# An agents' stage rebuilt ahead of four interleaved streams: sums' columns, masks, rows and step sequences

## The chip, the cores and the metric

The kernel runs on one core of one Trainium2 chip. The metric is the device time of one execution, in microseconds (us). The trace is one execution taken by the hardware profiler on that core. The engines are PE (TensorE matmuls; PEld is its loading of stationary operands), DVE (VectorE), ACT (ScalarE), POOL (GpSimd) and SP (SyncE), which here only issues DMAs. Each engine runs its own instructions in order and waits on semaphores for the others.

## The reference

Six layers with a residual and a layer norm after each, over x (32 batches, 100 tokens, 256 channels) and a context (32, 361, 256), all float32:

```
x = LN(x + L0_attn(x))              # the agents' layer
x = LN(x + L0_xattn(x, ctx, masks)) # cross attention with cell_mask and seq_mask
x = LN(x + L0_ffn(x))               # gate, top half of the tokens, 16-head attention
x = LN(x + L1_attn(x))              # banded 16-head attention
x = LN(x + L1_xattn(x, ctx))        # cross attention
x = LN(x + L1_ffn(x))               # quantised linear layer
```

The agents' layer is the one that the change rebuilds:

```
agent      = einsum('bnc,c->bn', q, w_conv1)            # one number a token
agent_attn = softmax(einsum('bn,bnc->bc', agent * scale, k))
agent_v    = softmax(einsum('bc,bnc->bn', agent_attn, v))
agent_v    = einsum('bn,bnc->bc', agent_v, v)           # one row of 256 a batch
agent_tok  = softmax(agent[:, :, None], axis=-1)
return agent_tok * agent_v[:, None, :]
```

The masks enter the first cross attention as `scores + log(cell_mask) + log(seq_mask)`.

## The kernel before, in words

**Streams and turns.** The 32 batches make 16 pairs. Four streams A, B, C, D take one pair each in a turn, and there are four turns. Each stream has its own SBUF tiles and its own two PSUM banks. A turn of a stream goes through the stages mix (adds the agents' rows, layer norm), first (cross attention with masks), pick (top half), local (banded attention), second (cross attention) and quant.

**Order.** For each engine a stream is a generator that yields after a step or a few. Strings of letters in `ORDER`, written out by a planner, say for PE, DVE, ACT, POOL and SP whose step is issued next. An engine works strictly in that order, so a step that waits holds up all that stand behind it.

**The agents' stage** comes before all turns and treats all 32 batches together. It has its own list of steps on each engine (`AGENT_TENSOR`, `AGENT_SCALAR`, `AGENT_VECTOR`), which the code calls by name:
- `w`: the vector w_q w_conv1, spread over the partitions (L299).
- `x0` to `x15`: tokens of four batches at a time (a "slot", eight slots) arrive by DMA and are transposed by PE (L320), two steps a slot; ACT copies them out. On DVE `ag0` to `ag7` give the agent numbers of a slot.
- `y0` to `y7`: the sums over tokens, agent times token, as rows (L327, output in four groups of 32 partitions); `row1` copies the four banks out (half on ACT, half on DVE); `yT1` turns the rows into columns (`rows_to_columns`, L307) and DVE copies them.
- `key`, `kmax`, `kexp`, `krec`, `kn`: scores of the first softmax, its maximum, exponential, reciprocal and division; `arT` transposes the result (L344), `z` multiplies by w_v (L349), and `log` gives the logits of the second softmax (L362).
- `lmax`, `lexp` (eight exponentials, L647), `lrec`, `ln` (L855 to L858): the second softmax; `col` turns it into columns (L385), `u0` to `u7` weigh the tokens again (L392), `row2`, `yT2` (L307 again) and `vec` give the agents' vector, copied out as step `v` (L871).
- `p0` to `p6`: products of weights that later stages use (L299, L354, L369, L374, L380), with a scaled copy each on DVE (L820, L822). They need nothing of the tokens.

After `v`, SP stores the 32 rows to DRAM (L1275), waits, and loads each stream's pair of rows over 100 partitions (L1225).

**Masks.** There is one room for the cell mask and one for the sequence mask (`cell`, `seq`), shared by all streams. POOL multiplies the two (L1158), DVE makes the "is zero" part and clips (L891, L893), ACT takes the logarithm (L665), POOL adds (L1162). The next stream's masks are loaded after that (L1229, L1230). So the four streams' masks of a turn follow one another. In the first turn they stand at the start of each stream's steps.

**POOL at the start.** It waits for `u7`, clears rows of the streams' work tiles (L1111, step `rows`, for which ACT and DVE wait before their turns), then clears the value tiles (L1117, L1118, step `zeros`).

## Time and profile before

| | us |
|---|---|
| median of 3 runs | 1081.24 |
| lowest and highest | 1078.39, 1082.4 |
| the profiled execution, its time | 1081.67 |
| its span in the trace | 1079.9 |
| PE busy in the span | 900.4 |
| DVE, ACT, POOL busy | 704.7, 514.2, 371.4 |

How to read it: "busy" counts time in which an engine has an instruction in work; matmuls overlap and their ends are modelled. The page's slices cut the span in 40 equal parts of 27 us; a digit is tenths. A window's row gives the stretch, its length, each engine's busy time with the number of instructions, the clock of PE that was granted (1.00 is 2.4 GHz, 0.50 is 1.2 GHz), the share of 16 DMA engines that was busy, and GB/s. A timeline's row gives start, duration (first start to last end), engine, line, operation, tiles, shape and count; in brackets the idle time before it and what ended that. An operation's row by source line gives count and the least, the median and the largest duration in ns. In the trace one f32 product of the kernel is two matmul instructions, a transpose one.

### The profile page before, as it was taken

Reading aid. Unit: us, or ns where it says so; the run is one execution under the profiler, and the core shown is the slowest. Engines: PE = TensorE matmul, PEld = TensorE weight load, DVE = VectorE, ACT = ScalarE, POOL = GpSimd, SP = SyncE. Lnnn points to the kernel's source line nnn. Section 1 sums busy time; section 2 is a strip of 40 time slices with the busy share of each in tenths; the row PEclk is TensorE's granted clock in tenths of the full one; section 3 lists DMA queues with packets and bytes.
Section 4 is the critical chain, followed back from the end, with each engine's and each line's share of the span. In section 5 each row is a group of like instructions: output and inputs, shape, how many; then the busy total and the mean of one; then the engine's idle time right before and its main releaser. Section 6 shows DMA issues by size and latency. Waiting matters only on the chain.

```text
span 1079.9 us, 19738 instructions
## 1 busy us (share of the span) xinstructions
PE 900.4 (83%) x7022; PEld 671.0 (62%) x7022; DVE 704.7 (65%) x2081; ACT 514.2 (48%) x2392; POOL 371.4 (34%) x528
## 2 busy tenths in 40 slices
PE   7957798898798699998889788897979688997983
PEld 5735677565577587665567566574647466765662
DVE  4235666565777857567697876558487686766576
ACT  3102244766542345865433355664535144556641
POOL 0045401344463322254443422236144232223243
PEclk9766898999888799997889699898869898998896
DMA  7801400002214000002032200011030400000000
GB/s 227 285 32 44 157 1 2 2 8 85 92 55 144 24 1 2 2 23 73 30 123 75 78 9 2 12 69 34 11 102 1 144 17 1 1 2 1 1 1 31
DMA packets 23382, 54.10 MB, mean 50 GB/s; under 512 B 3696, under 2 KB 9588, under 8 KB 23284
## 3 DMA queue, kind: packets, MB, share of 16 engines
q1 hardware_dynamic: 23284, 52.84, 14.7%
q8 instruction: 55, 0.90, 0.3%
q14 instruction: 43, 0.35, 0.1%
HBM read 49.53 MB, written 3.31 MB: 49 GB/s over the span
## 4 chain that ended last, share of the span: by engine, by line
PE 50%; DVE 26%; ACT 10%; POOL 5%; issue 4%; DMA 4%; SPq 1%; DVEq 0%; POOLq 0%; ACTq 0%
PE psum L419 8%; PE psum L424 8%; PE psum L458 7%; ACT work L763 4%; PE psum L444 4%; DVE bn L878 4%; PE psum L578 4%; PE psum L589 3%; ACT work L728 3%; DVE x L885 3%; PE psum L599 2%; DVE mx L1040 2%; PE psum L581 2%; DVE res L945 1%; DVE mv L880 1%
## 5 line engine op out<-in xcount | busy, mean ns | idle before, releaser
L763 ACT ACTIVATE work<-psum,mx 100x100 f32<-100x100 f32 x512 | 169.8, 369 | 53.1 <-DVE mx L1040 52.8
L1124 POOL TENSOR_SCALAR ve<-mv 100x2 f32<-100x2 f32 x96 | 21.7, 226 | 289.7 <-DVE mv L880 289.4
L763 ACT ACTIVATION_READ_ACCUMULATOR work<-psum,mx 100x1 f32 x512 | 118.5, 232 | 0.0
L657 ACT ACTIVATE xT<-psum 128x100 f32<-128x100 f32 (+3 forms) x144 | 53.0, 374 | 124.5 <-PE psum L594 55.9
L458 PE MATMUL psum<-eT,ctx 128*128 128x100 f32 x768 | 103.6, 292 | 7.0 <-DVE eT L914 6.7
L458 PEld LDWEIGHTS psum<-eT,ctx 128*128 128x128 f32 x768 | 99.6, 207 | 10.5 <-DVE eT L914 8.9
L1153 POOL COPY work<-rden 100x128 f32<-100x128 f32 (+1 forms) x80 | 25.1, 314 | 201.4 <-DVE rden L1044 172.6
L444 PE MATMUL psum<-ctxT,qT 128*100 128x361 f32 x256 | 92.6, 508 | 2.1 <-ACT qT L657 1.2
L657 ACT ACTIVATE eT<-psum 100x400 f32<-100x400 f32 (+3 forms) x128 | 64.1, 513 | 49.1 <-PE psum L617 21.2
L878 DVE BATCH_NORM_STATS2 bn<-res 100x6 f32<-100x256 f32 x192 | 82.1, 427 | 6.6
L1040 DVE TENSOR_REDUCE mx<-psum 100x4 f32<-100x400 f32 x128 | 66.9, 565 | 26.4 <-PE psum L581 26.2
L589 PE MATMUL psum<-ident,work 100*100 100x100 f32 x512 | 71.8, 273 | 14.1 <-ACT work L763 13.8
L885 DVE TENSOR_SCALAR x<-res,mv,rstd 100x256 f32<-100x256 f32 x160 | 73.5, 504 | 13.4 <-POOL rstd L1126 13.0
L728 ACT ACTIVATE work<-psum,mx 128x50 f32<-128x50 f32 x256 | 73.8, 349 | 16.4 <-DVE mx L999 16.3
L589 PEld LDWEIGHTS psum<-ident,work 100*100 100x100 f32 x512 | 54.5, 140 | 30.3 <-ACT work L763 22.8
L1126 POOL TENSOR_TENSOR rstd<-ve,minus_half 100x2 f32<-100x2 f32 x96 | 69.3, 722 | 8.0
L578 PE MATMUL psum<-kT,qT 64*100 64x400 f32 x256 | 64.5, 583 | 6.7 <-DVE aT L1051 6.6
L444 PEld LDWEIGHTS psum<-ctxT,qT 128*100 128x100 f32 x256 | 44.4, 181 | 36.0 <-issue 8.0
L1146 POOL TENSOR_TENSOR kT<-work,heads 128x400 f32<-128x400 f32 x64 | 54.4, 853 | 32.9 <-DVE work L1029 32.9
L728 ACT ACTIVATION_READ_ACCUMULATOR work<-psum,mx 128x1 f32 x256 | 63.3, 253 | 0.0
L1046 DVE COPY eT<-psum 100x400 f32<-100x400 f32 x64 | 35.5, 554 | 38.1 <-PE psum L589 37.8
L414 PE MATMUL psum<-ident,x 100*128 100x100 f32 x192 | 31.9, 294 | 28.7 <-DVE x L885 28.6
(231 smaller groups left out, 2066.3 us busy)
## 6 DMA issues: line engine op xcount, KB each, us to landing
ctx<-in_ctx SPq DMA_DIRECT2D x16, 768.0 KB, 7.0
ctxT<-in_ctxT SPq DMA_DIRECT2D x16, 722.0 KB, 4.3
cell<-in_cell SPq DMA_DIRECT2D x16, 282.0 KB
seq<-in_seq SPq DMA_DIRECT2D x16, 282.0 KB
x<-in_x SPq DMA_DIRECT2D x16, 200.0 KB
eT<-agent_rows SPq DMA_DIRECT2D x16, 200.0 KB
out<-xplus SPq DMA_DIRECT2D x16, 200.0 KB
work<-in_x SPq DMA_DIRECT2D x4, 400.0 KB
```

The costliest lines, as they stand in the source:

```text
L419: last = e.matmul(dst, w[:, c, h * P:(h + 1) * P], n(c), start=c == 0, stop=c == NC - 1)
L424: last = e.matmul(dst, xT(c), w[:, c, :], start=c == 0, stop=c == NC - 1)
L444: last = e.matmul(bk[b][0:S, 0:S2], s.qT[:, c, b * S:(b + 1) * S], s.ctxT[:, b, c, :], start=c == 0, stop=c == NC - 1)
L458: last = e.matmul(bk[b][:, c * S:(c + 1) * S], s.ctx[:, b, j, c * P:(c + 1) * P], s.pT[:, b, j, :], start=j == 0, stop=j == S2C - 1)
L578: e.matmul(bk[g][0:S, 0:4 * S], s.qT[r:r + 64, c, b * S:(b + 1) * S], s.keys[r:r + 64, i % 2, :, :], start=True, stop=False, skip_group_ch ...
L589: last = e.transpose(bk[g][0:S, q * S:(q + 1) * S], s.e[:, 4 * g + q, :], ident[0:S, 0:S])
L657: return e.activation(dst, src, ACT.Copy, **kw)
L728: last = e.activation(s.e_pick[:, 4 * g + i, j, 0:CAP], bk[g][:, at_:at_ + CAP], ACT.Exp, bias=s.mx[:, h:h + 1], accum_out=s.den[:, h:h + 1])
L763: last = e.activation(s.e[:, h, :], bk[g][0:S, q * S:(q + 1) * S], ACT.Exp, bias=s.mx[0:S, h:h + 1], accum_out=s.den[0:S, h:h + 1])
L878: e.bn_stats(s.bn[:, b, :], s.res[0:S, b, :]).then_inc(*dve.up(f"bn{b}"))
L885: e.tensor_scalar(dst[0:S, b, :], s.res[0:S, b, :], s.mv[:, b, 0:1], s.rstd[:, b:b + 1], ALU.subtract, ALU.mult).then_inc(*dve.up(f"x{b}"))
L1040: e.tensor_reduce(s.mx[0:S, 4 * g:4 * g + 4], bk[g][0:S, 0:4 * S].rearrange("p (h k) -> p h k", k=S), AX, ALU.max, negate=True).then_inc(* ...
```

## The change

1. *Sums' columns while tokens arrive.* The rows `y0` to `y7` and their turn into columns go. PE makes one column for each batch and half of the channels, with the batch's tokens as the stationary operand (`weighed`), a slot behind the transposes.
2. *Order of the agents' steps.* Only `p0` and `p2` stay ahead of the logits; `p1`, `p3` follow them, `p4` follows `u7`, `p5` and `p6` come last.
3. *Second softmax.* The maximum is subtracted by DVE (`sub0`, `sub1`), ACT takes two exponentials instead of eight; the division is done on the final vector, with a sum from one more matmul (`sum`, `rsum`).
4. *Masks of the first turn.* They are loaded early, into each stream's own tiles (`mask_rooms`), and worked on in the agents' stage: products first thing on POOL, clips on DVE after `row2` (A, B) and after `yT2` (C, D), logarithms on ACT after `row2`, sums on POOL. POOL's `rows` come after the sum of D.
5. *Agents' rows.* `agent_v` stays in SBUF; each batch's row is read from its partition by a DMA of its own over 100 partitions, eight in the first turn.
6. *Loads.* Constants in three groups (`ld_c`, `ld_first`, `ld_const`); the context of C and D after the agents' rows. The zeros of the value tiles move into POOL's first turn.
7. *Sequences.* All five strings of `ORDER` are new.

```diff
-AGENT_TENSOR = ("w " + " ".join(f"x{n}" for n in range(16)) + " " + " ".join(f"y{n}" for n in range(8))
-                + " yT1 key p0 p1 arT z p2 p3 log p4 p5 p6 col " + " ".join(f"u{n}" for n in range(8)) + " yT2 vec")
+AGENT_TENSOR = ("w x0 x1 " + " ".join(f"x{2 * n} x{2 * n + 1} y{n - 1}" for n in range(1, 8)) + " y7 key p0 arT z p2 log p1 p3 "
+                "col sum " + " ".join(f"u{n}" for n in range(8)) + " p4 yT2 vec p5 p6")
...
+            def weighed(i, weights):
+                for j in range(ROWS):
+                    b = ROWS * i + j
+                    for c in range(NC):
+                        last = e.matmul(psum[:, 7, c * B + b:c * B + b + 1], x_of(b)[:, c * P:(c + 1) * P],
+                                        weights[:, b:b + 1], start=True, stop=True)
+                return last
...
-                last.then_inc(*agent_pe.up(f"y{i}"))
-            e.wait_ge(*agent_act("row1"))
-            e.wait_ge(*agent_dve("row1"))
-            rows_to_columns().then_inc(*agent_pe.up("yT1"))
...
+                if i:
+                    e.wait_ge(*agent_dve(f"ag{i - 1}"))
+                    weighed(i - 1, ag).then_inc(*agent_pe.up(f"y{i - 1}"))
...
-            e.wait_ge(*agent_dve("lmax"))
-            for i in range(SLOTS):
-                last = e.activation(l_rooms[i // 4][:, i % 4, :], psum[:, i // 4, i % 4 * P:i % 4 * P + S], ACT.Exp,
-                                    bias=lstat[:, 0, i:i + 1], accum_out=lstat[:, 1, i:i + 1])
+            for k in range(2):
+                e.wait_ge(*agent_dve(f"sub{k}"))
+                last = e.activation(l_rooms[k], l_rooms[k], ACT.Exp)
...
+            for s in streams:
+                masks_log(e, s, 0)
...
+            for s in streams[2:4]:
+                masks_clip(e, s, 0)
             e.wait_ge(*agent_pe("vec"))
-            e.tensor_copy(agent_v, psum[0:B, 6, 0:D]).then_inc(*agent_dve.up("v"))
+            e.tensor_scalar(agent_v[:, :], psum[0:B, 6, 0:D], astat[:, 3:4], None, ALU.mult).then_inc(*agent_dve.up("v"))
+            product(wqk[:, :, :].rearrange("p c n -> p (c n)"), 5, 5)
+            product(wvo[:, :, :].rearrange("p c n -> p (c n)"), 4, 6)
+            e.wait_ge(ld_first, LD_FIRST)
...
         def gpsimd_agents(e):
+            for s in streams:
+                masks_product(e, s, 0)
+            for s in streams:
+                masks_sum(e, s, 0)
+            e.wait_ge(*SD.gpsimd["mask"]("sum", 0))
             e.wait_ge(*agent_pe("u7"))
             for s in streams:
                 last = e.memset(s.work[32 * (ROWS - 1):P, 0:H * HALF], 0.0)
             last.then_inc(*agent_pool.up("rows"))
...
         def load_agent(e, s, t):
-            e.dma_start(s.agent.rearrange("p b d -> p (b d)"),
-                        agent_rows[s.pair(t):s.pair(t) + 1, :].to_broadcast([S, NB * D])).then_inc(s.load_agent.sem, 16)
+            for b in range(NB):
+                n = NB * s.pair(t) + b
+                e.dma_start(s.agent[:, b, :], agent_v[n:n + 1, :].unsqueeze(1).to_broadcast([1, S, D])).then_inc(s.load_agent.sem, 16)
...
             e.wait_ge(*agent_dve("v"))
-            e.dma_start(agent_rows.rearrange("n (b d) -> (n b) d", b=NB), agent_v).then_inc(agent_kept, 16)
-            e.wait_ge(agent_kept, 16)
             for s in streams:
                 load_agent(e, s, 0)
+            for s in (SC_, SD):
+                load_ctx(e, s, 0)
...
     "DVE": (
-        "AAABBAABAACCABCABABABADDCACDBBCCABBADDBABCDCCBDACBABDCDACDABDDBCDCBACABDADDCABDACABABDCABCADBABDCABA"
+        "DBACABDCAABCBADCBDACABCBADCABDACBABCDADBCDBACDCBADBACDBCAACDBADBADCBBCDABCABCADBADABDBABCCDABCABACBD"
```

## Rows read from the trace of the kernel before

**Rows 1.** The page: span, PE's clock in 40 slices, one group of instructions.
```profile
span 1079.9 us, 19738 instructions
...
PEclk9766898999888799997889699898869898998896
...
L657 ACT ACTIVATE eT<-psum 100x400 f32<-100x400 f32 (+3 forms) x128 | 64.1, 513 | 49.1 <-PE psum L617 21.2
```

**Rows 2.** Windows of the fill and of the turns.
```profile
83.00:95.00 12.00, 8.68 (x20) 5.27 (x20) 7.00 (x10) 2.61 (x7) 6.32 (x5) 0.61 0.15 45
...
83.06:200.00 116.94, 98.47 (x771) 79.20 (x772) 69.94 (x223) 50.32 (x234) 36.43 (x43) 0.86 0.13 46
200.00:1000.00 800.00, 686.68 (x5395) 508.04 (x5399) 552.88 (x1602) 415.31 (x1972) 293.56 (x420) 0.89 0.12 41
...
400.00:500.00 100.00, 91.36 (x856) 67.38 (x857) 64.50 (x186) 65.64 (x339) 37.86 (x54) 0.98 0.07 25
```

**Rows 3.** Transposes by source line in three stretches, and windows of two of them.
```profile
6.70:22.30 15.60, 12.81 (x69) 10.39 (x72) 12.21 (x66) 7.57 (x15) 0.00 (x0) 1.00 0.84 261
...
98.00:101.20 3.20, 3.20 (x17) 3.20 (x17) 0.00 (x0) 0.35 (x1) 3.20 (x3) 0.50 0.00 0
...
L320 PE MATMUL psum<-ident,work x32: 374/374/430, 6.7 to 13.3; 100*128 100x100 f32 x32
...
L414 PE MATMUL psum<-ident,x x4: 374/374/374, 100.3 to 100.8; 100*128 100x100 f32 x4
...
L414 PE MATMUL psum<-ident,x x4: 249/276/308, 111.0 to 111.4; 100*128 100x100 f32 x4
```

**Rows 4.** L307 on PE's timeline, whole and its last 19, and a window.
```profile
29.41 5.54 PE L307 MATMUL psum<-ident,v 128*128 128x4 f32 x32 [0.92 <-DVE v L813]
...
30.85 4.10 PE L307 MATMUL psum<-ident,v 128*128 128x4 f32 x19
...
31.00:33.00 2.00, 2.00 (x11) 2.00 (x11) 0.00 (x0) 0.00 (x0) 0.00 (x0) 0.50 1.02 337
```

**Rows 5.** PE's timeline: the transposes of the last tokens.
```profile
20.71 1.59 PE L320 MATMUL psum<-ident,ctxT 100*128 100x100 f32 x8 [1.10 <-DMA ctxT<-in_x]
```

**Rows 6.** PE's timeline around the agent's softmax.
```profile
38.98 1.91 PE L299 MATMUL psum<-res,c_bk_c 128*128 128x256 f32 x4
41.84 0.31 PE L344 MATMUL psum<-ident,kT 32*128 32x32 f32 x2 [0.95 <-DVE kT L840]
```

**Rows 7.** DVE's and PE's timelines, from the logits to their columns.
```profile
49.39 0.99 DVE L848 TENSOR_REDUCE kT<-psum 128x8 f32<-128x800 f32 x1 [4.29 <-PE psum L362]
...
54.73 1.06 DVE L858 TENSOR_TENSOR qT<-qT,kT 128x400 f32<-128x400 f32 x2
...
55.84 1.58 PE L385 MATMUL psum<-ident,qT 128*100 128x4 f32 x16 [1.99 <-DVE qT L858]
```

**Rows 8.** Timelines of POOL, DVE and ACT, from `u7` to the first turn.
```profile
63.14 3.90 POOL L1111 MEMSET work<- 32x1024 f32 x4 [62.70 <-PE psum L392]
...
69.91 0.23 DVE L869 COPY kT<-psum 128x64 f32<-128x64 f32 x1 [4.65 <-PE psum L307]
...
77.95 0.54 DVE L893 TENSOR_SCALAR cell<-cell 100x722 f32<-100x722 f32 x1
78.40 0.48 DVE L945 SCALAR_TENSOR_TENSOR res<-eT,tok,x 100x256 f32<-100x256 f32 x1
78.60 0.81 ACT L665 ACTIVATE cell<-cell 100x722 f32<-100x722 f32 x1 [17.12 <-DVE cell L893]
...
79.49 2.01 POOL L1162 TENSOR_TENSOR kT<-cell,kT 100x722 f32<-100x722 f32 x1 [2.22 <-ACT cell L665]
...
80.42 0.18 DVE L880 BATCH_NORM_AGGREGATE mv<-bn 100x2 f32<-100x6 f32 x1
...
81.76 0.71 POOL L1126 TENSOR_TENSOR rstd<-ve,minus_half 100x2 f32<-100x2 f32 x1
```

**Rows 9.** A window while the agents' rows are loaded.
```profile
76.00:78.00 2.00, 0.00 (x0) 0.00 (x0) 0.59 (x2) 0.00 (x0) 1.27 (x1) 0.50 0.59 207
```

More of the change, by code:

```diff
@@ L92 @@
 GPSIMD = {
+    "start": "zeros",
     "mask": "prod sum",
@@ L351, in tensor_agents @@
             last.then_inc(*agent_pe.up("z"))
-            spread(4, cols["c_bv"], W["c_o"]).then_inc(*agent_pe.up("p2"))
-            for c in range(NC):
-                last = e.matmul(psum[:, 5, 0:1], cols["c_bk"][:, c:c + 1].to_broadcast([P, P]), cols["c_bq"][:, c:c + 1],
-                                start=c == 0, stop=c == NC - 1)
-            last.then_inc(*agent_pe.up("p3"))
+            spread(5, cols["c_bv"], W["c_o"]).then_inc(*agent_pe.up("p2"))
             e.wait_ge(*agent_dve("zT"))
@@ L371, in tensor_agents @@
             last.then_inc(*agent_pe.up("p4"))
+            e.wait_ge(*agent_act("row2"))
+            e.wait_ge(*agent_dve("row2"))
+            for c in range(NC):
+                for i in range(SLOTS):
+                    at_ = (c * SLOTS + i) * ROWS
+                    last = e.matmul(psum[:, 7, at_:at_ + ROWS], u_rooms[i // 2][:, i % 2, c * P:(c + 1) * P],
+                                    ident[:, 0:P:32], start=True, stop=True)
+            last.then_inc(*agent_pe.up("yT2"))
+            e.wait_ge(*agent_dve("yT2"))
+            for c in range(NC):
+                last = e.matmul(psum[0:B, 6, 0:D], yT[:, c, :], W["w_v0T"][:, c, :], start=c == 0, stop=c == NC - 1)
+            last.then_inc(*agent_pe.up("vec"))
+            e.wait_ge(*agent_dve("p3"))
             for h in range(NC):
@@ L623, in tensor_turns, with masks_log @@
                 yield
+        def masks_log(e, s, t):
+            part = mask_rooms(s, t)[0]
+            e.wait_ge(*s.vector["mask"]("clip", t))
+            e.activation(part, part, ACT.Ln).then_inc(*s.scalar["mask"].up("ln"))
         def scalar_agents(e):
             e.preload_act_table_set("natural_log_exp_and_others")
-            def row(name, first, last_, scale):
-                for k, after in ((0, first), (1, last_)):
-                    e.wait_ge(*agent_pe(after))
-                    last = e.activation(y_rooms[k].rearrange("p i d -> p (i d)"), psum[:, k, :], ACT.Copy, scale=scale)
-                last.then_inc(*agent_act.up(name))
             for n in range(NC * SLOTS):
@@ L661, in tokens_columns @@
                 copy(s.xT[:, :, :].rearrange("p c t -> p (c t)"), bk[0][:, 0:NC * T]).then_inc(*act.up("xT"))
-            def masks(t):
-                e.wait_ge(*s.vector["mask"]("clip", t))
-                e.activation(cell[:, :, :], cell[:, :, :], ACT.Ln).then_inc(*s.scalar["mask"].up("ln"))
             def cross(t, stage, bq):
@@ L808, in vector_agents @@
             e.tensor_tensor(tokd, ag, ag, ALU.subtract).then_inc(*agent_dve.up("tokd"))
-            def row(name, first, last_, scale):
-                for k, after in ((2, first), (3, last_)):
-                    e.wait_ge(*agent_pe(after))
-                    last = e.tensor_scalar(y_rooms[k].rearrange("p i d -> p (i d)"), psum[:, k, :], scale, None, ALU.mult)
-                last.then_inc(*agent_dve.up(name))
             def product(dst, k, n, other=None):
@@ L861, in vector_agents @@
+            product(wqbk[:, :], 4, 1)
+            product(bqbk[:, :], 5, 3)
             e.wait_ge(*agent_pe("col"))
             e.tensor_copy(acol, psum[0:S, 7, 0:B]).then_inc(*agent_dve.up("acol"))
-            row("row2", "u5", "u7", 1.0)
-            e.wait_ge(ld_const, LD_CONST)
+            e.wait_ge(*agent_pe("sum"))
+            e.reciprocal(astat[:, 3:4], psum[0:B, 6, D:D + 1]).then_inc(*agent_dve.up("rsum"))
+            for k, ready in ((2, "u5"), (3, "u7")):
+                e.wait_ge(*agent_pe(ready))
+                last = e.tensor_copy(u_rooms[k][:, :, :].rearrange("p i d -> p (i d)"), psum[:, k, :])
@@ L865, in vector_agents @@
+            last.then_inc(*agent_dve.up("row2"))
+            product(bqk[:, :], 4, 4)
+            for s in streams[0:2]:
+                masks_clip(e, s, 0)
             e.tensor_scalar(bq4[:, :], cols["a_bq"][:, :], HEAD_SCALE, None, ALU.mult)
@@ L1112, in gpsimd_agents @@
             last.then_inc(*agent_pool.up("rows"))
-            e.wait_ge(*agent_pool("rows"))
-            e.wait_ge(*agent_dve("w8"))
-            e.wait_ge(*agent_pe("yT2"))
-            for s in streams:
-                e.memset(s.v_pick[:, :, :, :], 0.0)
-                last = e.memset(s.v[:, :, :, :], 0.0)
-            last.then_inc(*agent_pool.up("zeros"))
+            e.wait_ge(ld_first, LD_FIRST)
         def gpsimd_turns(e, s):
```

325 lines of the change are left out of this document (156 added, 169 removed).

## The prediction

> **What bounds the kernel now.** I read the page first. PE is the busiest engine, and its slices of granted clock drop below full speed often [rows 1]. The windows cut the span in three. Up to 83.06 us the agents' stage runs alone. From 83.06 to 200 the four streams fill up: PE is busy 98.5 of 116.9 us at a mean clock of 0.86, so it does 84.7 us of full-clock work. From 200 to 1000 it is busy 686.7 of 800 at 0.89, or 0.764 us of full-clock work per us [rows 2]. At that rate the work before 200 would have taken 110.9 us, so the fill loses only 6.0 us. This is the first thing to see. The masks that come one after the other look bad (the first chain waits for them: PE is busy 8.7 of 12 us at 0.61 [rows 2]), but freeing them can give back about 6 us, not the 40 us by which the streams start apart.
>
> The second thing is the level of PE's clock while the tokens arrive. The clock slices say 9 there, but the matmuls say otherwise. The transposes of that stage take 374 ns each. The same form takes 374 ns where the granted clock is 0.50 (1.2 GHz), and 249 ns at the least where it is 1.00 (2.4 GHz) [rows 3]. So the stage runs at 1.2 GHz. I trust the durations over the slices.
>
> The third is the price of a matmul with few columns. In the turn of rows into columns (L307), 32 of them take 5.54 us, and the 19 that start after 30.85 take 4.10, which is (4.10 - 0.35) / 18 = 0.208 us apart at clock 0.50. The 13 before them start in 30.85 - 29.41 = 1.44 us, 0.111 apart [rows 4]. The load of the 128 stationary columns sets this, so a single column costs as much as four.
>
> **The change, part by part.**
>
> *Sums' columns while tokens arrive.* The 64 matmuls that made rows (L327, 22.3 to 28.6), their copies, and the 32 of L307 go. In their place stand 64 products, one column each, with the tokens as stationary operand. Every f32 product of this kernel is two instructions in the trace (16 calls of L307 are x32), so 128 instructions. They stand in PE's queue between the transposes. The last tokens arrive at 20.7 us; eight transposes take 1.59 us [rows 5], so (1.59 - 0.37) / 7 = 0.17 each. New PE work: 64 x 0.17 + 128 x 0.208 = 10.9 + 26.6 = 37.5 us from 6.7 us, plus 0.5 us for the second group of tokens and some 0.4 us of turnover. The last sum is there at 45.2 us. The old one was there at 29.41 + 5.54 = 34.95 [rows 4]: **+10.2 us**. The transposes wait behind these products, but nobody wants them before the logits. Bounds: below, the products cost what the transposes with the same stationary tile cost (0.17), which takes 4.9 us off; above, 0.208. I take the upper one, since L307's form is nearest.
>
> The Trainium skill ("TensorE: Matmul & The Clock Gate", LDWEIGHTS) has a load of 128 columns take 107 ns whatever the contraction. By it the products would cost 128 x 0.107 = 13.7 us, 12.9 less. The row of L307 at the low level, 0.208, disagrees for f32, and the row decides.
>
> *Agent's softmax.* p1 leaves the path: its four matmuls (38.98, 1.91 us) stood before the transpose of the normalised row at 41.84 [rows 6]. That starts 2.6 us sooner relative to the key. Against this, p0 is dense for only half as long, and before, the clock rose to 1.00 after p0 and p1. I let z, p2 and the logits run at the low level: 8 x 0.1 + 4 x 0.2 + about 1 for the logits, less 0.5 for p3, is +2.1, an estimate from the two spacings (bounds 0 and 3). Net -0.5.
>
> *Second softmax.* From the logits' end (49.39) to the columns (55.84) it was 6.45 us: eight exponentials, then DVE was late with p6 and two products of 0.53 [rows 7]. Now: maximum 0.99, two subtractions of about 0.55, the second exponential of 400 columns 0.51 [rows 1], waits 0.2, so 2.8 us. p1 and p3 lie under it. **-3.6 us.** The missing division moves to a scalar of the last copy. The sum over tokens adds 0.3, and p4 (eight matmuls of one column, 0.9 us at full clock by L307's spacing) stands where only a copy of 0.6 stood: +0.3. Copies, u and the second turn into columns stay.
>
> So far 10.2 - 0.5 - 3.6 + 0.6 = +6.7 us: the agents' vector is there 6.7 us later, near 79.
>
> *Masks of the first turn and zeros.* POOL idled 62.7 us before L1111 [rows 8], so the four products cost nothing; without that cover 1.7 us each. But the tail of the chain is now on the path. DVE clips C and D after the columns' copy (done at 70.14 before, 76.8 now): four of 0.54, done at 79.0. ACT takes the logarithm, 0.81. POOL adds C, then D (2.0 at most each), near 82.3, and only then clears the streams' rows, which took 3.90 [rows 8] when they lay under the second turn into columns. ACT and DVE wait for this signal before any turn: 86.3. Two other chains end close by. PE's p5 and p6 are 16 matmuls at (1.91 - 0.63) / 3 = 0.43 us at the low level, 6.9 us after 79, then 0.7 on DVE: 86.6 at worst. The agents' rows are eight DMAs: issue 8 x 0.4, and the bytes of before moved at 207 GB/s (0.82 MB in 4 us [rows 9]) after some 1.3 us: 85 to 86. DVE's first turn thus starts at 86.4 where it started at 78.40: +8.0. The HBM hop that falls away (about 1.5 us) is hidden behind the other two. If DVE's clips and POOL's sums slow each other, up to 3 more.
>
> *New sequences.* DVE's now begins D, B, A, C. A mix takes 2.2 us. Two others before A's are 4.4; C's before A's normalisation covers POOL's two steps (1.0 with the wait, 81.46 to 82.47) and costs 1.2; A no longer waits for its mask's sum (79.49 + 2.01 against 80.6 [rows 8]), -0.9. PE's first transpose of a stream: 83.06 + 8.0 + 4.7 = 95.8, **+12.7 us**. From there all four streams are ready within 3 us and no mask is waited for. The 6.0 us of fill come back, less some 2.0 for the first 5 us at the low level (0.43 a us against 0.764): **-4.0 us**. Context of C and D is issued behind the agents' rows at about 84 and needs 11 us at the rate of A's and B's: it is wanted after 98, hidden. The zeros now stand in POOL's turns, 1.4 a stream in 20 us that have room.
>
> The rest of the sequences changes everywhere. No row prices that: 989 us of turns keep their work. I take nothing, with +-1% as bounds. PE's last eight steps are all of D, where C and D ended together; up to 5 us of loss.
>
> **Sum.** 1079.9 + 12.7 - 4.0 = 1088.6 us of span. The profiled execution took 1081.67, 1.8 more than its span; the median 1081.24 is 0.4 less. So 1088.6 + 1.8 - 0.4 = **1090.0 us**, slower by 0.8%.
>
> **Rivals.**
> *The turns run denser (faster).* With four streams ready at once and no mask between them, PE may run its first 100 us as it did from 400 to 500: 91.4 busy at 0.98, 0.90 a us against 0.764 [rows 2]. That is 100 x (0.90 / 0.764 - 1) = 17.5 us: 1090 - 17.5 = 1072.5. It decides from 14 us on. For it: PE waits for nobody else there. Against: before, the streams' distance is what mixes their stages, and now they start in step.
> *PE at full clock while tokens arrive.* Then all of it costs half: a group of 8 transposes and 16 products 2.4 us, more than the tokens' arrival still, and the sums end near 28.5: -16.7, so 1073. Against it: the transposes kept PE busy 12.8 of 15.6 us and the level stayed low; L307's back-to-back products let it fall from 1.00 [rows 3, 4].
> *The agents' rows come one packet at a time.* Each DMA reads one partition a hundred times. Before, the source was DRAM: 0.59 of 16 engines for 2 us moved 414 KB, 0.046 us of an engine per KB [rows 9]. In series, 800 KB take 37 us instead of 4. D's rows are the last issued and the first that DVE wants, so all turns wait: up to +32, and 1090 + 32 = 1122. Nothing in the trace reads one partition so; one row of DRAM read a hundred times was no bottleneck.
> The Trainium skill ("SBUF — State Buffer", the DMA port swizzle) gives a port 27.2 GB/s and puts partitions 0 to 3 behind one port: 0.82 MB would take 30 us, some 25 more than I count, 1115 us. No row here shows it.
> *The change only trades.* Denser turns by half of the above: 1081.
>
> **Chances.** Forecast 0.44 (own range 1083 to 1097); denser turns 0.15; only trades 0.12; full clock 0.07; rows in series 0.22 (wholly or in part, 1100 to 1122). The range 1070 to 1115 leaves out about 0.15. 0.5% is about what a measurement can tell, 1075.8 to 1086.6. Faster: 0.15 and 0.07 less their upper edges, 0.19. Same: 0.12, 0.10 of the forecast's low side, and those edges, 0.24. Slower: 0.57.
>
> **What would show it.** Products of one column 0.2 us apart between transposes of 374 ns; the sums' copy on DVE near 45; the vector's copy near 79; clear of rows on POOL from 82; DVE's first mix at 86 and released by POOL (if by the agents' DMA and near 115, the series rival); PE's first transposes near 96; then PE busy over 90% to 150. I am wrong if the level is 1.00 in the token stage, or if the windows after 200 move by over 1%.

## The result, and the profile after

The changed kernel takes 1112.47 us (median of 4 runs: 1104.71, 1105.9, 1119.05, 1120.25) against 1081.1 for the one before on the same chip: ratio 1.0297, interval 1.025 to 1.0345. The profiled execution took 1104.71 us, its span is 1102.9, 23.0 more than before. The forecast was 1090.0; the time lies in the forecast's range, but by the rival with the agents' rows in series and not by the case that I held likeliest.

Columns are those of before: start, duration, engine, line, operation, tiles, shape, count, and idle time with its releaser. First the page, to set against [rows 1].

```profile
span 1102.9 us, 19819 instructions
...
PEclk7675889999898889999899998998969969999696
```

PE's timeline of the token stage and around the agent's vector, to set against [rows 4 to 7]:

```profile
9.78 1.87 PE L314 MATMUL psum<-qT,work 100*128 100x1 f32 x16
...
15.52 1.57 PE L327 MATMUL psum<-ident,work 100*128 100x100 f32 x8
16.88 3.46 PE L314 MATMUL psum<-qT,work 100*128 100x1 f32 x16
...
35.63 6.87 PE L314 MATMUL psum<-qT,ctxT 100*128 100x1 f32 x32
...
111.89 1.56 PE L425 MATMUL psum<-ident,x 100*128 100x100 f32 x8 [36.74 <-DVE x L900]
```

The products of one column stand between the transposes, 3.46 us for 16. The last ends at 42.50 (before: 34.95). What no row of before resembles is the last line: PE idles 36.7 us before the turns' first transposes, which start at 111.89 instead of 83.06. DVE's timeline says for what:

```profile
70.65 0.47 DVE L883 TENSOR_SCALAR agent_v<-psum,vs 32x256 f32<-32x256 f32 x1
...
75.18 0.69 DVE L830 TENSOR_SCALAR wvo<-psum 128x512 f32<-128x512 f32 x1 [1.45 <-PE psum L411]
...
102.90 0.48 DVE L950 SCALAR_TENSOR_TENSOR res<-eT,tok,x 100x256 f32<-100x256 f32 x1 [27.03 <-DMA eT<-agent_v]
...
111.36 2.66 DVE L900 TENSOR_SCALAR x<-res,mv,rstd 100x256 f32<-100x256 f32 x5
```

The vector is there at 70.65, 1.5 us *earlier* than before (72.15). Then DVE waits 27.03 us for a DMA, and does 8.5 us of residuals and statistics of all four streams before it normalises one. The DMA queue's own timeline (SP) and the window of the stretch:

```profile
71.15 23.21 SPq L1241 DMA_DIRECT2D eT<-agent_v  x8
94.40 3.94 SPq L1250 DMA_DIRECT2D ctxT<-in_ctxT  x1
98.39 2.97 SPq L1252 DMA_DIRECT2D ctx<-in_ctx  x1
```

```profile
74.00:98.00 24.00, 1.14 (x6) 0.66 (x4) 0.69 (x1) 0.00 (x0) 3.63 (x5) 0.64 0.46 28
...
220.00:1024.00 804.00, 674.37 (x5434) 498.47 (x5436) 560.99 (x1608) 416.20 (x1985) 299.99 (x425) 0.92 0.15 41
```

The eight copies need 23.2 us only to be issued, where a DMA is otherwise issued in 0.4, and the last column of the window says what they move: 28 GB/s, where the loads before the turns moved 207 [rows 9]. 800 KB at this rate are some 30 us. One other thing shows in the waits of the whole run: in the turns DVE's residual waits for the next `x`, 18.7 us in three waits. Before it was 6.7 in two.

```profile
DVE res L950 <- DMA eT<-agent_v: 27.0, 1, 27.0
DVE res L950 <- DMA x<-in_x: 18.7, 3, 8.5
```

### The profile page after: what moved, and what is told of

It is laid out like the page before. It is cut to its first block and busy times, and to the rows that moved or that the text cites. A ratio compares the mean times of both kernels' runs of the same rounds, so it can differ in the third digit from the quotient of the medians.

```text
span 1102.9 us, 19819 instructions
## 1 busy us (share of the span) xinstructions
PE 890.6 (81%) x7056; PEld 669.8 (61%) x7056; DVE 713.3 (65%) x2079; ACT 508.8 (46%) x2376; POOL 374.2 (34%) x528
## 5 line engine op out<-in xcount | busy, mean ns | idle before, releaser
L671 ACT ACTIVATE xT<-psum 128x400 f32<-128x400 f32 (+3 forms) x144 | 53.8, 380 | 157.6 <-PE psum L425 96.5
L770 ACT ACTIVATION_READ_ACCUMULATOR work<-psum,mx 100x1 f32 x512 | 123.4, 246 | 0.0
L469 PE MATMUL psum<-eT,ctx 128*128 128x100 f32 x768 | 98.9, 284 | 7.3 <-DVE eT L922 6.9
L469 PEld LDWEIGHTS psum<-eT,ctx 128*128 128x128 f32 x768 | 94.8, 200 | 11.0 <-DVE eT L922 8.8
L900 DVE TENSOR_SCALAR x<-res,mv,rstd 100x256 f32<-100x256 f32 x160 | 85.4, 578 | 15.5 <-POOL rstd L1141 15.1
L455 PE MATMUL psum<-ctxT,qT 128*100 128x361 f32 x256 | 90.3, 498 | 5.7 <-ACT qT L686 4.4
L602 PE MATMUL psum<-ident,work 100*100 100x100 f32 x512 | 68.9, 267 | 23.4 <-ACT work L770 23.3
L425 PEld LDWEIGHTS psum<-ident,x 100*128 100x128 f32 x192 | 23.6, 160 | 62.0 <-issue 38.4
```

Of the source, the lines that this page charges most:

```text
L455: last = e.matmul(bk[b][0:S, 0:S2], s.qT[:, c, b * S:(b + 1) * S], s.ctxT[:, b, c, :], start=c == 0, stop=c == NC - 1)
L469: last = e.matmul(bk[b][:, c * S:(c + 1) * S], s.ctx[:, b, j, c * P:(c + 1) * P], s.pT[:, b, j, :], start=j == 0, stop=j == S2C - 1)
L602: last = e.transpose(bk[g][0:S, q * S:(q + 1) * S], s.e[:, 4 * g + q, :], ident[0:S, 0:S])
L671: return e.activation(dst, src, ACT.Copy, **kw)
L770: last = e.activation(s.e[:, h, :], bk[g][0:S, q * S:(q + 1) * S], ACT.Exp, bias=s.mx[0:S, h:h + 1], accum_out=s.den[0:S, h:h + 1])
L900: e.tensor_scalar(dst[0:S, b, :], s.res[0:S, b, :], s.mv[:, b, 0:1], s.rstd[:, b:b + 1], ALU.subtract, ALU.mult).then_inc(*dve.up(f"x{b}"))
```

## The experiments

Eleven kernels ran, one of them twice. The theories that the trace of the changed kernel suggests: **S**, the copies are slow since they all read the same few partitions; **Q**, they are slow since something else occupies the DMA engines; **O**, the loss is in the new sequences. Here are the results together; "vector" and "first transposes" are starts in the profiled execution of each, in us. Ratios are to the kernel before on the same chip; its median there lay between 1078.5 and 1082.7, so a difference between medians of two rows is good to a few us.

| kernel | median | ratio (interval) | vector | first transposes | span |
|---|---|---|---|---|---|
| before | 1081.24 | 1 | 72.15 | 83.06 | 1079.9 |
| changed | 1112.47 | 1.0297 (1.025 to 1.0345) | 70.65 | 111.89 | 1102.9 |
| k1: rows by DRAM | 1071.49 | 0.9911 (0.9876 to 0.9946) | 70.34 | 87.77 | 1068.4 |
| k11: only the first turn from SBUF | 1094.62 | 1.0137 (1.0088 to 1.0186) | 70.44 | 113.17 | 1092.6 |
| k10: only later turns from SBUF | 1090.33 | 1.0086 (1.0054 to 1.0118) | 75.28 | 94.16 | 1092.2 |
| k4: k1 with sequences of before | 1078.38 | 0.9963 (0.9929 to 0.9998) | 70.20 | 81.34 | 1071.1 |
| k9: changed, sequences of before | 1098.59 | 1.0185 (1.0135 to 1.0235) | 73.27 | 89.69 | 1091.3 |
| k3: before, first turn from SBUF | 1098.81 | 1.0223 (1.0146 to 1.03) | 70.60 | 88.24 | 1094.2 |
| k2: k1 with sums of before | 1060.47 | 0.9857 (0.9801 to 0.9913) | 66.07 | 83.83 | 1055.8 |
| k2 again | 1061.77 | 0.9837 (0.9788 to 0.9885) | 63.10 | 81.35 | 1059.6 |
| k12: k2, DVE's start changed | 1062.81 | 0.9829 (0.979 to 0.9868) | 68.03 | 79.94 | 1060.8 |
| k6: copies in another order | 1097.75 (one run) | | 75.54 | 104.20 | 1096.0 |
| k8: copies as D, B, A, C | 1098.54 (one run) | | 74.61 | 106.44 | 1096.7 |
| k7: half of each row | 1078.32 (one run) | | 73.69 | 100.60 | 1076.5 |

### The agents' rows by DRAM, all else changed (k1)

```diff
-            for b in range(NB):
-                n = NB * s.pair(t) + b
-                e.dma_start(s.agent[:, b, :], agent_v[n:n + 1, :].unsqueeze(1).to_broadcast([1, S, D])).then_inc(s.load_agent.sem, 16)
+            e.dma_start(s.agent.rearrange("p b d -> p (b d)"),
+                        agent_rows[s.pair(t):s.pair(t) + 1, :].to_broadcast([S, NB * D])).then_inc(s.load_agent.sem, 16)
...
             e.wait_ge(*agent_dve("v"))
+            e.dma_start(agent_rows.rearrange("n (b d) -> (n b) d", b=NB), agent_v[:, :]).then_inc(agent_kept, 16)
+            e.wait_ge(agent_kept, 16)
```

> The changed kernel with one part undone: the agents' vector is stored to DRAM and each stream's [100, 512] tile is loaded from there with one DMA, as in the kernel before; all else stays changed. Theory S (the eight SBUF copies all read the same few partitions, and that is what made them last from 71 to 103 us): the DMAs are over within 4 to 8 us of the issue, the first transposes of the turns start near 86 to 90 instead of 111.9, and about 6 us of the 23 to 25 gained are lost again since the fill has less time to give back: 1079 to 1088. Rival Q (the copies were slow because the weights', masks' and contexts' loads of the changed order lie on the same DMA engines at that time): the DRAM version is late too, first transposes after 100, total above 1095. Rival O (the loss is in the new step sequences, and the late start would have been made up): first transposes early, but the total above 1095. The measured times of the changed kernel fell into two groups, 1105 and 1120; if these come from the SBUF copies, this kernel has one group, within 3 us.

1071.49 us, 0.9911 of the kernel before: with this one part undone the change is a gain, of 0.9%. DVE's and the DMA queue's timelines:

```profile
70.34 0.47 DVE L885 TENSOR_SCALAR agent_v<-psum,vs 32x256 f32<-32x256 f32 x1
...
78.78 0.48 DVE L952 SCALAR_TENSOR_TENSOR res<-eT,tok,x 100x256 f32<-100x256 f32 x1 [3.23 <-DMA eT<-agent_rows]
...
87.24 2.66 DVE L902 TENSOR_SCALAR x<-res,mv,rstd 100x256 f32<-100x256 f32 x5
```

```profile
70.83 0.32 SPq L1296 DMA_DIRECT2D agent_rows<-agent_v  x1
72.29 1.44 SPq L1241 DMA_DIRECT2D eT<-agent_rows  x4
73.77 0.36 SPq L1251 DMA_DIRECT2D ctxT<-in_ctxT  x1
```

The wait for the rows shrinks from 27.03 to 3.23 us, and the contexts of C and D are issued at 73.8 instead of 94.4. The same loads stand before and behind, so theory Q falls. The start, 87.77, is as expected. The total is 8 to 16 us lower than expected: the spans differ by 34.5 us, the starts by only 24.1. So some 10 us more lay in the turns; k10 looks there. The times of this kernel spread over 1066.8 to 1082.4, so the expectation of one narrow group failed too.

### Which bytes, which partitions (k7, k6)

k7 leaves out the second half of each row.

```diff
-                e.dma_start(s.agent[:, b, :], agent_v[n:n + 1, :].unsqueeze(1).to_broadcast([1, S, D])).then_inc(s.load_agent.sem, 16)
+                e.dma_start(s.agent[:, b, 0:P], agent_v[n:n + 1, 0:P].unsqueeze(1).to_broadcast([1, S, P])).then_inc(s.load_agent.sem, 16)
```

> The changed kernel with each agent copy cut to its first 128 of 256 columns, 512 B a packet instead of 1 KB (it leaves out the other half of the agent's row). Theory by bytes (the source is read at about 26 GB/s): the eight copies take 15 to 17 us instead of 30, the first transposes start near 97, total near 1090. Theory by packet (0.30 us a packet whatever its size, for instance a turn-round or a conflict at the source): 28 to 32 us, first transposes near 110, total 1100 to 1107.

```diff
-            for s in streams:
-                load_agent(e, s, 0)
+            for s, b in ((SA, 0), (SC_, 0), (SA, 1), (SC_, 1), (SB_, 0), (SD, 0), (SB_, 1), (SD, 1)):
+                n = NB * s.pair(0) + b
+                e.dma_start(s.agent[:, b, :], agent_v[n:n + 1, :].unsqueeze(1).to_broadcast([1, S, D])).then_inc(s.load_agent.sem, 16)
```

> The changed kernel with only the order of the eight copies of the first turn changed: A row 0, C row 0, A row 1, C row 1, then B and D in the same way, so that neighbouring copies read partitions 0 to 3 and 4 to 7 in turn. Theory S1 (each copy is held to the rate at which one group of four partitions is read, about 26 GB/s, and the groups are independent): the eight are over in half to two thirds of the 30 us, 15 to 20 us after the issue, first transposes of the turns near 98 to 102, total 1090 to 1100. Theory S2 (one rate for all of them, whichever partition they read): 30 us as before, first transposes within 2 us of 111.9, total 1100 to 1110 (or its second group, 1120).

In the trace the 800 packets of the changed kernel run from 72.64 to 102.42 (29.8 us), those of k7, half as large, from 75.67 to 91.19 (15.5 us): bytes count, not packets, 27.5 and 26.4 GB/s. In k6 they run from 77.53 to 94.77, 17.2 us. The windows of k7 and then of k6, in the middle of the copies (last column GB/s):

```profile
77.00:89.00 12.00, 2.44 (x9) 1.67 (x8) 1.38 (x2) 0.00 (x0) 3.67 (x5) 0.78 0.41 27
```

```profile
80.00:92.00 12.00, 0.00 (x0) 0.00 (x0) 0.34 (x1) 0.00 (x0) 2.58 (x3) 0.65 0.51 53
```

27 GB/s with rows 0 to 7 in order; 53 with nothing changed but that neighbouring copies read a row of 0 to 3 and a row of 4 to 7. The limit is not the destination either, since k1 fills the same tiles. So it stands at the source, one for each of two groups of rows, and S is shown. The DMA share says how: 0.46 of 16 engines, 7 of them, were in work in the changed kernel and 0.51 in k6, nearly the same, but a KB took 0.46 x 16 / 28 = 0.26 us of an engine there and 0.51 x 16 / 53 = 0.15 in k6, where it took 0.046 from DRAM before [rows 9]. The packets did not go one at a time; several were under way at once, and each was slow. The first transposes come 26.9 us (k7) and 28.7 us (k6) after the vector, against 41.2. The Trainium skill ("SBUF — State Buffer", the DMA port swizzle) puts partitions 0 to 3 behind one port and 4 to 7 behind another, at 27.2 GB/s a port; the traces agree with 27.5, and with 53 for two. No run here tries other pairs of partitions.

The vector itself came at 73.7 and 75.5 here, though its stage is the same; see the clock below. k7's total, 1078, is 12 us under its expectation, though its start is 3.6 us later than expected; the copies of later turns are halved too, which may be why (k10 prices them).

### The order of the streams (k8)

```diff
-            for s in streams:
+            for s in (SD, SB_, SA, SC_):
                 load_agent(e, s, 0)
```

> The changed kernel with only the order of the streams in the eight copies changed, to D, B, A, C, which is the order in which VectorE's sequence takes them. Theory M (VectorE does all four streams' residuals and statistics before the first normalisation, 2.1 us a stream, so all eight rows are needed at once, and only the work of three streams is drawn under the copies): first residual near 80 instead of 102.9, the last stream's still at 103, first transposes of the turns 105 to 106 instead of 111.9, total 6 us less than 1104.7, about 1098. Rival M2 (the mismatch of the two orders was the trouble, and the first stream can start alone): first transposes near 88 to 92, total near 1085.

1098.54 us, 6.2 under the changed kernel's 1104.71, as theory M gave. From the vector to the first transposes it is 31.8 us instead of 41.2 (6.3 were expected from three streams' work; the copies also last 26.7 us instead of 29.8, which may be since D's rows and B's lie in different groups). In DVE's timeline the first residuals of the four streams start at 84.86, 93.39, 98.72 and 103.78, each behind a wait for its rows; the first and the last:

```profile
84.86 0.48 DVE L950 SCALAR_TENSOR_TENSOR res<-eT,tok,x 100x256 f32<-100x256 f32 x1 [4.43 <-DMA eT<-agent_v]
...
103.78 0.48 DVE L950 SCALAR_TENSOR_TENSOR res<-eT,tok,x 100x256 f32<-100x256 f32 x1 [2.85 <-DMA eT<-agent_v]
```

That D's rows came last was the small part of it. The sequence wants all eight rows before anything is normalised, and the last stream's residual still starts at 103.78.

### Is it the sequence? (k3, k9, k4)

The old sequences want the streams' rows one after another: residuals at 78.40, 91.09, 104.63 and 120.95 in the trace of before. Copies at 7.5 us a stream would be in time for all but the first. So I expected the slow copies to cost 1 to 6 us there.

k3 is the kernel before with this edit:

```diff
+            for b in range(NB):
+                n = NB * s.pair(t) + b
+                row = (agent_rows[s.pair(t):s.pair(t) + 1, b * D:(b + 1) * D].to_broadcast([S, D]) if t else
+                       agent_v[n:n + 1, :].unsqueeze(1).to_broadcast([1, S, D]))
+                e.dma_start(s.agent[:, b, :], row).then_inc(s.load_agent.sem, 16)
```

> The kernel before with one thing changed: the agents' rows of the first turn are copied by eight DMAs out of SBUF, a row at a time, in the order A, B, C, D; the store to DRAM and its wait stay, and later turns read from there. Theory B (the copies are held to 26 to 27 GB/s, 7.5 us a stream, and what they cost depends on how many streams are needed at once): the rows are there at about 81, 89, 96 and 104, and the sequences of before want them at 78.4, 91.1, 104.6 and 121, so only stream A's 3 us are lost: first transposes 85 to 87 instead of 83.1, total 1082 to 1087 against 1081.5. Rival B2 (the series costs its 30 us wherever it stands, for instance since everything behind it in the queue is late too): total above 1095. Rival B3 (nothing is lost, the fill gives the 3 us back): 1080 to 1082.

k9 is the changed kernel, k4 is k1, both with `ORDER` of before, cut to the steps that are left:

```diff
     "DVE": (
-        "DBACABDCAABCBADCBDACABCBADCABDACBABCDADBCDBACDCBADBACDBCAACDBADBADCBBCDABCABCADBADABDBABCCDABCABACBD"
+        "AABAABAACABCABABADCACDBBCCABBADDBABCDCCBDACBABDCDACDABDDBCDCBACABDADDCABDACABABDCABCADBABDCABACCAB"
```

> The changed kernel, agents' rows from SBUF as there, with the turns' step sequences of the kernel before (cut to the steps that are left, the first turn's clearing put into GpSimd's). Theory B (the SBUF copies cost so much only because the new sequences want all four streams' rows before the first transposes): stream A's rows are there near 79 to 80 and the first transposes start 83 to 86 instead of 111.9; the later turns' copies still cost a few us; total 1080 to 1092, that is 15 to 30 us less than the changed kernel. Rival B2 (30 us wherever): first transposes after 100, total 1100 or more.

> As the kernel with the agents' rows from DRAM again, and with the turns' step sequences of the kernel before (cut to the steps that are left; the first turn's clearing put into GpSimd's). It measures what the new sequences are worth when the agents' rows come in time. Theory S: the sequences are worth under 1% either way, 1075 to 1095; the old ones begin with stream A's work and want A's masks first, so the first transposes of the turns start 85 to 90. Rival O (the new sequences are fitted to agents' rows that are early and cost time in the body): this kernel is at least 8 us faster than the one with the new sequences. Rival N (the new sequences are denser, and they gave back what the turns after 220 us show, busy TensorE 669 us against 687 in the same 800): this kernel is at least 8 us slower than it.

k3 takes 1098.81, 1.0223 of before, 20 to 24 us more; I had expected 1 to 6. My theory B fell, and its rival B2 holds in kind, at 20 us and not 30: what stands behind the copies is late. The start is late by 5.2 us only (88.24, against 85 to 87 in theory B). The rest is in POOL's and the DMA queue's timelines of k3:

```profile
106.43 1.70 POOL L1158 TENSOR_TENSOR cell<-cell,seq 100x722 f32<-100x722 f32 x1 [18.79 <-DMA seq<-in_seq]
```

```profile
72.51 23.12 SPq L1229 DMA_DIRECT2D eT<-aT  x8
95.68 3.91 SPq L1232 DMA_DIRECT2D cell<-in_cell  x1
```

The rows of B, C and D were in time; only A's residual waited for its own, 7.4 us. What stood behind them was not in time: stream B's mask was issued at 95.68 instead of 81.52, POOL waited 18.79 us for it, and B's residual ran at 111.18 instead of 91.09. These 20.1 us stay: the stores of the output stand 19 to 21 us later than before in all but the last four, and 14 to 15 there.

k9 tells the same of the changed kernel: 1098.59, where k4, with rows by DRAM, takes 1078.38; 20.2 us for the copies. Its start after the vector is 5.3 us later than k4's (16.4 against 11.1), and the waits for the next `x` are 23.2 us against 8.1. I had expected 1080 to 1092, so theory B missed here as well. k9 is also 14 us faster than the changed kernel, and the two intervals do not meet. So the old sequences suffer less from the copies, and the new ones, with the rows in time, do no worse than the old: 1071.49 against 1078.38, 6.9 us, intervals that meet at 0.993 to 0.995. Rival O is out; that the new ones are better by themselves is likely and not settled.

### First turn and later turns apart (k11, k10)

k10 and k11 are k1 with the condition of k3's edit as `t == 0` and as `t` (DRAM where it holds), and with a DMA for each row, where k1 has one for a stream's two.

> The other half: the first turn's rows from SBUF, the later turns' from DRAM. Theory F (the first turn pays by the start of the turns, 111.9 against 87.8): first transposes near 112, total 21 to 26 us over the kernel with DRAM rows alone, 1092 to 1097. Rival F2 (part of the late start is given back in the fill, and the later copies cost more than the waits for x show): total under 1088.

> The changed kernel with the first turn's agents' rows from DRAM and those of the turns after from SBUF (eight and twenty-four copies, a row each; the second DMA of a stream reads the other half of the DRAM row). It measures what the slow copies cost once the turns run. Theory L (behind them in the queue stand the next x, which VectorE's residual waits for: 18.7 us in three waits in the changed kernel against 7.5 with all rows from DRAM): first transposes near 88, the waits for x 17 to 19 us in sum, total 9 to 13 us over the kernel with DRAM rows alone (median 1071.5, profiled 1070.2). Rival L2 (these waits are taken up by slack): total within 3 us of it. Sum rule: with the next kernel's cost it should give 34.5, the difference of the two profiled times.

k11 costs 23.1 us over k1 and k10 18.8, 41.9 together; the changed kernel costs 41.0 over k1. By the medians they add up. The spans of the profiled executions do not: 24.2 and 23.8 are 48.0, against 34.5. k10's profiled execution was one of its slowest (1093.96 of 1086.95 to 1095.93) and the changed kernel's its fastest, so I go by the medians, and the sum is good to several us. In k11 the late start, 25.4 us, arrives at the end almost whole (24.2 in the span): the turns give next to nothing back. k10's 18.8 is more than I expected (9 to 13). Its waits:

```profile
DVE res L952 <- DMA x<-in_x: 19.1, 3, 8.5
POOL xplus L1147 <- DMA out<-xplus: 6.5, 1, 6.5
DVE res L952 <- DMA eT<-agent_rows: 5.1, 1, 5.1
```

and k1's:

```profile
DVE res L952 <- DMA x<-in_x: 7.5, 3, 5.7
...
POOL xplus L1147 <- DMA out<-xplus: 2.5, 1, 2.5
```

11.6 us for the next `x` and 4.0 for a store's end are 15.6; the profiled run of k10 also had its vector 4.9 us later. Nobody waits for a later row itself. The copies hurt what is queued behind them, as in the DMA queue's timeline of the changed kernel:

```profile
870.74 1.54 SPq L1241 DMA_DIRECT2D eT<-agent_v  x2
872.39 3.66 SPq L1236 DMA_DIRECT2D x<-in_x  x1
876.10 3.09 SPq L1321 DMA_DIRECT2D out<-xplus  x1
```

In k1 the same two were issued in 0.30 each.

### The sums of before (k2), and a start for DVE (k12)

k2 is k1 with the wide sums of before, their copies and L307's turn into columns back; the masks of C and D are loaded after `yT1`, since the rows stand in their tiles.

```diff
-                if i:
-                    e.wait_ge(*agent_dve(f"ag{i - 1}"))
-                    weighed(i - 1, ag).then_inc(*agent_pe.up(f"y{i - 1}"))
...
+            for i in range(SLOTS):
+                e.wait_ge(*agent_dve(f"ag{i}"))
+                for j in range(ROWS):
+                    b = ROWS * i + j
+                    last = e.matmul(psum[32 * j:32 * j + 32, i // 2, i % 2 * D:(i % 2 + 1) * D],
+                                    ag[:, b:b + 1].to_broadcast([S, 32]), x_of(b), start=True, stop=True)
```

> The changed kernel with two parts undone: the agents' rows go through DRAM, and the token sums are again the 32 wide matmuls behind all transposes with their copies and the 16 small matmuls into columns (their rooms: the tiles of the two products of weights, and two v tiles, for which the masks of streams C and D are loaded after the columns). The rest of the change stays. It measures what the sums' columns cost. Theory T (they cost what the trace of the changed kernel shows, last token matmul at 42.5 instead of 35, and all of it lies on the path to the agents' vector): vector at 63 to 66 instead of 70.3, first transposes of the turns 81 to 85 instead of 87.8, total 4 to 7 us under the kernel with DRAM rows alone (1071.5): 1064 to 1068. Rival P (GpSimd's mask sums and clearing, which end at 77.4, hold the start instead): first transposes 86 to 88, total within 2 us of 1071.5. Rival C (the columns cost nothing net, since the wide way lacks the time for copies and columns at the end and meets the clock at half speed): vector at 68 to 71, total within 2 us.

> The kernel with DRAM rows and the old way of the token sums once more, beside the next one and with more rounds, for its gain over the kernel before and as what the next one stands against. By its first look (1060.5, ratio 0.986) 1056 to 1064 and a ratio between 0.98 and 0.99. Were that first ratio a matter of the chip, it would come out near 0.99, which is what the kernel with DRAM rows alone gave.

1060.47 and 1061.77 us; ratios 0.9857 and 0.9837. That is 10 us under k1 (6 to 8 by the ratios, whose intervals still touch k1's), and under the 1064 to 1068 that theory T had. The vector comes at 66.07 and 63.10 (68.03 in k12, same stage), 65.7 in the mean; in the nine kernels with the columns it comes at 70.20 to 75.54, 72.7 in the mean. The difference of 6.9 us is near that of the last sum, 42.50 against 34.95 before. Theory T holds in its mechanism, and P falls: POOL's sums and clearing moved up with the vector. The windows of the token stage of the second run of k2 stand against the changed kernel's: 

```profile
8.00:35.00 27.00, 21.90 (x162) 16.28 (x161) 13.30 (x68) 9.38 (x19) 0.00 (x0) 0.97 0.75 220
```

```profile
7.20:42.50 35.30, 35.26 (x193) 34.65 (x191) 12.21 (x66) 8.06 (x17) 6.83 (x4) 0.57 0.82 251
```

In the changed kernel PE works 35.3 us without a gap; in k2 it works 21.9 of 27. The clock of 0.97 in k2's row is not borne out: up to 24 us eight of its transposes take 1.60 us, the time of 0.50 [rows 3, 5]. The columns take more of it than the copies and small matmuls which they replace.

```diff
     "DVE": (
-        "DBACABDCAABC
+        "ABADBCDCAABC
```

> The kernel just named with eight steps of VectorE's sequence changed: it began D B A C (residual and statistics of all four streams) and then A B D C (their normalisations); now A B A D B C D C, so that A is normalised after two streams' statistics instead of four. Theory V (the first transposes wait for VectorE's eight residuals in a row, 74.8 to 83.3): they start 4 us earlier, 79 to 80, and 2 to 4 us of that are seen in the total: 1056 to 1059. Rival V2 (the other streams' normalisations then come later by what A's comes earlier and TensorE, which wants A B A D, stalls): total within 2 us of its neighbour. Rival V3 (GpSimd takes A, B and D's reciprocal roots first and then A's sum of rows, so C's start slips): slower by 1 to 3 us.

1062.81, no difference that the intervals tell. The first transposes do come earlier, 11.9 us after the vector instead of 18.3. But then PE waits for the others:

```profile
79.94 0.90 PE L439 MATMUL psum<-ident,x 100*128 100x100 f32 x4 [6.16 <-DVE x L922]
82.59 0.93 PE L439 MATMUL psum<-ident,x 100*128 100x100 f32 x4 [1.75 <-DVE x L922]
```

In k2's second run both streams' eight transposes went in one piece at 81.35. From the vector to the end of the span it is 992.8 us here, 996.5 and 989.7 in the two profiled runs of k2. The median is where rival V2 had it, and PE's waits are of its kind; but V's 2 to 4 us are within the noise, so it can't be ruled out.

## Why the prediction was right or wrong

**The agents' rows: the step that failed.** It said: eight DMAs, issue 8 x 0.4, and then the rate of before, 207 GB/s [rows 9], so that the rows are there at 85 to 86. They moved at 27.5, issue alone took 23.2 us, and the first mix ran at 102.90. I took the nearest rate of the trace, but that was of loads whose source is DRAM. A rival at 0.22 had the outcome, all rows behind one slow read, with 800 KB in series in 37 us; it was 29.8. Its mechanism was right in part: many reads of one partition are slow, but not since the packets go one at a time at the old 0.046 us a KB. Some 7 engines worked at once, and a KB took each 0.26 us. That the two prices lie so close is luck. The step had a second error: "up to 32" priced the start alone. The same copies in later turns cost 18.8 us (k10), because of what is queued behind them; I had costed what stands behind them for the first turn's contexts, but not for the later turns' `x`.

**Sums' columns: mechanism right, size 2.7 us too large in this execution.** Forecast 45.2 for the last, measured 42.50, so +7.5 and not +10.2. The products at the low level (0.50, 1.2 GHz) take 3.46 us for 16: less the 0.35 of one, (3.46 - 0.35) / 15 = 0.207 apart, my 0.208 [rows 4]. But the first 16 ran at 1.00 and took 1.87, (1.87 - 0.25) / 15 = 0.108 apart. The Trainium skill ("TensorE: Matmul & The Clock Gate", LDWEIGHTS) gives a load's time as its columns / 1.2 in ns, 107 ns for 128 columns as an estimate; that fits this row at 2.4 GHz, and at 1.2 GHz the rows show twice that. In k10's execution all the products took 3.46 us for 16, the time of the low level, and the last sum ended at 38.88 + 6.87 = 45.75, as forecast. (The windows print 1.00 for this stretch of k10, as they do for the token stage of before; here too I go by the durations.) PE's timeline of k10:

```profile
10.76 3.46 PE L316 MATMUL psum<-qT,work 100*128 100x1 f32 x16
...
38.88 6.87 PE L316 MATMUL psum<-qT,ctxT 100*128 100x1 f32 x32
```

The full-clock rival is out in all of them.

**Softmaxes: direction right, too small.** From the last sum to the vector I forecast 3.5 us less; it was 70.65 - 42.50 = 28.15 against 72.15 - 34.95 = 37.20, 9.05 less. Some of this is the clock: it was granted at 1.00 from 46.4 to 56.6, and the logits took 3.0 us instead of 4.5; the second turn into columns took 3.7 instead of 5.92. Those two are 3.7 us; the other 1.9 beyond the forecast's 3.5 are not traced. "Near 79" for the vector is wrong by 8 us in all.

**Masks, clearing, D-B-A-C.** I had 9.4 us from DVE's first mix to the first transposes (86.4 to 95.8). With the rows by DRAM it is 78.78 to 87.77, 9.0. POOL's clearing there ended 7.0 us after the vector; I had 7.3:

```profile
73.77 3.61 POOL L1134 MEMSET work<- 32x1024 f32 x4
```

These steps held, but for which one ends last: in k1 it is the rows (78.78), 1.4 us behind the clearing (77.38). The start without the copies is +4.7 us instead of +12.7, and the 8.0 between are the vector's 8.6.

**The turns: "nothing taken", -4.0 for the fill.** In k1 the start is 4.7 us later and the end 11.5 earlier, so the turns gave back 16.2. My rival "the turns run denser" had 17.5, and said that it decides from 14. PE's windows of k1, from the start to 220 and after, against before [rows 2]:

```profile
87.80:220.00 132.20, 122.00 (x1031) 95.65 (x1033) 83.63 (x251) 69.34 (x346) 43.28 (x61) 0.93 0.01 2
...
220.00:1024.00 804.00, 686.05 (x5418) 501.61 (x5415) 565.42 (x1632) 416.12 (x1979) 299.25 (x427) 0.90 0.13 42
```

122.0 x 0.93 / 132.2 is 0.858 us of full-clock work a us. The fill runs above the rate of before's turns (0.764), so my reading that it can give back no more than the 6.0 it loses was the mistake: I had taken the later turns' mean as the ceiling. k4 splits it. With the old sequences the start is 1.7 us earlier and the end 8.8, so 7.1 come without the new sequences and 9.1 with them. That the 7.1 are the masks' being out of the way is not shown by itself, and the split is of one execution each: by the medians the sequences are worth 6.9. My sign for the turns, windows after 200 that move by over 1%, came up: from 200 to 1000 PE is busy 670.6 us at 0.92 in the changed kernel, against 686.7 at 0.89 [rows 2]. In full-clock work that is about 1% more.

**Sum.** Forecast of the span: 12.7 - 4.0 = +8.7. Measured: +4.7 for the start without the copies, -16.2 in the turns, +34.5 for the copies (k1's span to the changed one's): +23.0. Two large terms of opposite sign were missed, one of them a gain. By the medians the copies cost 41, and the profiled execution was the fastest of the changed kernel: against its median the forecast of 1090.0 is 22.5 us short.

**Open.** The changed kernel's times lie in two groups, near 1105 and near 1120, and k1's spread over 15 us as well. One cause can be seen. Nine kernels with the same stage have the vector from 70.20 to 75.54. Where it is early (four of them, 70.20 to 70.65), the first products ran at 1.00 and the last sum ends at 41.8 to 42.5; in k8, k9 and k10 they took the time of 0.50 and it ends at 45.0 to 45.8. k7 and k6 had fast first products too (last sum 41.6 and 43.2), but the stretch of 44 to 52 us was granted 0.50 in both, against 0.85 in the changed kernel, and their vectors come at 73.69 and 75.54. The stretch of 60 to 66 us was granted 1.00 in the changed kernel and 0.50 in k10. That makes 5 us. The other 10 are not explained.

## What to carry to other kernels

Before a broadcast is sourced from SBUF, ask how many partitions it reads: a row that is read a hundred times cost all its copies' bytes at 27.5 GB/s here, and the hop through DRAM delayed the loads' issue by 1.5 us (70.83 to 72.29 in k1). Price a slow DMA not by who waits for it but by what is behind it on its queue: in k3 all rows but the first stream's were in time, and their neighbour, a mask, cost 20 us. And a change of many parts should be measured part by part: here two parts lose 41 and 6 to 10 us, and what is left is 1.5% faster than the kernel before (1060.5 to 1061.8 us).

## What the runs showed of the hardware

- Copies out of partitions 0 to 7 of a tile, a row each: 27.5 GB/s in order, 53 when neighbouring copies alternate between 0 to 3 and 4 to 7, with 0.46 and 0.51 of the 16 DMA engines busy. By DRAM the same bytes took 8 us from the store's issue (70.83) to the residual that wants D's, the last issued (78.78).
- A slow DMA holds the issuing queue: eight issues took 23.2 us instead of 8 x 0.4, and the two loads behind them 3.94 and 2.97.
- One-column products with 128 stationary columns in f32: 0.108 us apart at clock 1.00, 0.207 at 0.50, both in one execution of one stage.
- The same stage in nine kernels ended up to 5.3 us apart (70.20 to 75.54), with the place where the higher clock was granted: 44 to 52 us at 0.85 with the vector at 70.65, at 0.50 with 75.54 (k6).
